# A Flamingo block on one core: statistics, scaling, transposes, routing and shared expert of each mixture put into one block, quad by quad

## What is computed

```python
x = x + tanh(g_xattn[0]) * L0_xattn(layernorm(x), ctx)
x = x + tanh(g_ffn[0])   * moe0(layernorm(x))      # stage b of the kernel
x = x + tanh(g_xattn[1]) * L1_xattn(layernorm(x), ctx)
x = x + tanh(g_ffn[1])   * block1(layernorm(x))    # stages d (attention) and e (mixture)

# moe0: 64 experts in 8 groups, 4 groups kept, 6 experts per token, and a shared expert
shared = silu(x @ sg_w.T) * (x @ su_w.T) @ sd_w.T
scores = sigmoid(x @ gate_w.T) + gate_bias
masked_scores = scores * mask_of_the_4_best_groups
topk_w, topk_i = top_k(masked_scores, 6); topk_w /= sum + 1e-8 ; comb = scatter(topk_w)
routed = einsum(silu(x eg) * (x eu), ed, comb)
# second half of block1: 8 experts, 2 per token, no shared expert
t = rmsnorm(x, g2); probs = softmax(t @ router_w); w = top2(probs) / sum
y = sum_e w_e * (silu(t w1_e) * (t w3_e)) w2_e ;  return res + y
```

## Time and profile before

| | us |
|---|---|
| median of 3 runs (2174.27 to 2177.08) | 2176.98 |
| the profiled execution | 2178.36 |
| its span (first to last instruction) | 2176.6 |
| PE busy | 1817.9 (84%) |
| DVE busy | 1544.9 (71%) |
| POOL busy | 1145.5 (53%) |
| ACT busy | 1067.9 (49%) |

### The profile page before, as it was taken

How to read it: one execution, slowest core, us unless ns; L and a number is a source line. 1 busy time by engine, 2 the same in 40 slices (tenths; PEclk the granted TensorE clock), 3 DMA queues, 4 the chain that set the end, 5 groups by cost and what they waited for, 6 DMA issues and landing times. The chain is left out here.

```text
span 2176.6 us, 40812 instructions
## 1 busy us (share of the span) xinstructions
PE 1817.9 (84%) x12306; PEld 1455.1 (67%) x12306; DVE 1544.9 (71%) x3089; ACT 1067.9 (49%) x2730; POOL 1145.5 (53%) x1146
## 2 busy tenths in 40 slices
PE   4677844699999999957999999994688884399998
PEld 3455533488888888846999999993444443388886
DVE  5698869477777777776666666665578785487776
ACT  2366632255555555534655665561256662255554
POOL 4666621476676677643333333334567762276664
PEclk9699965799999999977999999996889995599999
DMA  5111100355556555400000000000000000122222
GB/s 120 44 45 40 38 1 17 90 129 144 143 144 144 138 133 146 127 19 4 5 3 3 3 3 3 3 3 0 0 2 1 0 1 2 50 68 78 78 68 68
DMA packets 99989, 114.75 MB, mean 53 GB/s; under 512 B 18448, under 2 KB 55504, under 8 KB 99888
## 3 DMA queue, kind: packets, MB, share of 16 engines
q1 hardware_dynamic: 93888, 110.96, 19.8%
q10 hardware_dynamic: 6000, 2.57, 0.6%
HBM read 101.82 MB, written 3.28 MB: 48 GB/s over the span
## 5 line engine op out<-in xcount | busy, mean ns | idle before, releaser
L76 POOL TENSOR_TENSOR b_moe_hid_low<-b_moe_hid,b_moe_hid_high 128x512 fp32r<-128x512 f32 x256 | 331.4, 1295 | 168.1 <-ACT b_moe_hid_high L1007 166.4
L1013 ACT ACTIVATE bank<-bank 128x512 f32<-128x512 f32 x384 | 223.5, 582 | 368.4 <-PE bank L83 368.4
L1547 POOL TENSOR_TENSOR c_prob<-c_prob,c_recip 128x480 f32<-128x480 f32 x128 | 126.2, 986 | 308.0 <-DVE c_recip L1698 308.0
L1656 ACT ACTIVATE c_prob<-bank,c_shift 128x120 f32<-128x120 f32 x512 | 177.5, 358 | 183.2 <-DVE c_shift L1690 183.2
L1038 DVE TENSOR_TENSOR b_moe_gu<-bank,XC 128x512 f32<-128x512 f32 x256 | 176.7, 690 | 108.5 <-PE bank L83 107.4
L76 POOL TENSOR_TENSOR e_moe_hid_low<-e_moe_hid,e_moe_hid_high 128x512 fp32r<-128x512 f32 x128 | 165.7, 1295 | 84.4 <-ACT e_moe_hid_high L1007 83.6
L71 DVE CAST c_ts_high<-bank 128x480 fp32r<-128x480 f32 x128 | 84.9, 663 | 165.9 <-PE bank L1578 165.9
L1043 DVE TENSOR_TENSOR b_moe_hid<-bank,b_moe_gu 128x512 f32<-128x512 f32 x256 | 177.0, 691 | 8.8 <-POOL b_moe_hid_low L76 0.2
L1007 ACT ACTIVATE b_moe_hid_high<-b_moe_hid 128x512 fp32r<-128x512 f32 x256 | 159.9, 625 | 5.7 <-DVE b_moe_hid L1043 5.1
L1578 PE MATMUL bank<-c_cs,mT 96*128 96x120 f32 x1024 | 138.8, 280 | 6.2 <-POOL c_wvp_low L76 4.9
L1578 PEld LDWEIGHTS bank<-c_cs,mT 96*128 96x128 f32 x1024 | 133.1, 196 | 14.9 <-POOL c_wvp_low L76 5.3
(11 more groups left out here) (367 smaller groups left out, 5455.9 us busy)
## 6 DMA issues: line engine op xcount, KB each, us to landing
XC<-b_comb SPq DMA_DIRECT2D x256, 256.0 KB, 4.3
...
```

Source lines behind the costliest of these rows:

```text
L76: return eng.tensor_tensor(low.bitcast(F32R), x, high, ALU.subtract)
L1013: act.activation(gate_b[j % 4][:], gate_b[j % 4][:], ACT.Silu).then_inc(s_silu, 1)
L1547: pool.tensor_tensor(prob[k][:], prob[k][:], recip[:, k, :].unsqueeze(2).broadcast_to([P, HG, NKV]), ALU.mult).then_inc(s_norm, 1)
L1656: i = act.activation(prob[k][:, h, :], score_b[g % 2][:, h * NKV:(h + 1) * NKV], ACT.Exp, bias=shift[:, k, h:h + 1], accum_out=sums[:, k, ...
```

## The change

`stats`, `Norm` and `route` are replaced, for the two mixtures, by one function `settle` with one block. In it each quad goes through all its steps, and every loop is written out.

- DVE: `bn_stats` of quad t, `bn_aggr` of quad t-1, variance of quad t-2 (and mean square of quad t-3 in stage e), all eight quads; then the routing chain of the eight quads without anything between. The subtraction over 4096 columns and the scaling leave DVE. In stage b the addition of the bias and the last multiplication of the chain go to Pool, and "not equal" and "times" become one `scalar_tensor_tensor` (in stage e too).
- ACT: scales (in stage b with the shift as bias), four instructions a quad; then both copies of the quad before, and the sigmoid or exponential of the one before that. After all eight quads it turns to a second loop: `stage` copies and the shared expert's activations.
- Pool: per quad the power and (stage b) the shift, the low part, the bias addition, the last multiplication; then in the same list the shared expert's weights, its product and its low part. In stage e it adds Z (scaled by ACT) to X in eight pieces.
- PE: transposes and logits of all quads; then, quad by quad, the shared expert's first two products, the transposes of the routing weights, and the third product of the quad before. Gate and up have one PSUM bank each.
- SP: the four stores of routing weights of each quad, instead of ACT.

The diff, cut:

```diff
-        def route(tag, ctx, XT, combD, s_stored, norm, gateT, ne, logits_to_scores, comb):
...
+        def settle(tag, ctx, src, centred, gain, XT, combD, s_stored, gateT, ne, comb, scores, shared=None):
...
+                @block.sync
+                def _(sp):
+                    for q in range(NQ):
+                        sp.wait_ge(s_cc, q + 1)
                         for j in range(4):
                             per = P // width
                             rows = (j % per) * width
-                            act.dma_start(combD[:, bass.ds(q * 512 + j * P, P)],
-                                          stage[u][rows:rows + ne, (j // per) * P:(j // per + 1) * P]).then_inc(s_stored[u], 16)
-                    body(0, 0)
-                    body(1, 1)
-                    with stepped(act, 2, NQ, 2) as q:
-                        store_comb(q - 2, 0)
-                        body(q, 0)
-                        store_comb(q - 1, 1)
-                        body(q + 1, 1)
-                    store_comb(NQ - 2, 0)
-                    store_comb(NQ - 1, 1)
+                            sp.dma_start(combD[:, q * 512 + j * P:q * 512 + (j + 1) * P],
+                                         stage[q % 2][rows:rows + ne, (j // per) * P:(j // per + 1) * P])\
+                                .then_inc(s_stored[q % 2], 16)
                     for k in range(2):
-                        act.wait_ge(s_stored[k], 32 * NQ)
+                        sp.wait_ge(s_stored[k], 32 * NQ)
...
+                    for t in range(NQ + 3):
+                        if t < NQ:
+                            tile_stats(t)
+                        if 0 <= t - 1 < NQ:
+                            gather_stats(t - 1)
+                        if 0 <= t - 2 < NQ:
+                            variance(t - 2)
+                        if 0 <= t - 3 < NQ:
+                            mean_square(t - 3)
+                    dve_scores(dve)
...
+                    def roots(q):
+                        part = slice(4 * q, 4 * q + 4)
+                        pool.wait_ge(s_var, q + 1)
+                        pool.tensor_tensor(rstd[:, part], var[:, part], root[:], ALU.pow).then_inc(s_rs, 1)
+                        if centred:
+                            pool.wait_ge(s_rs, q + 1)
+                            pool.tensor_tensor(shift[:, part], negmean[:, part], rstd[:, part], ALU.mult).then_inc(s_shift, 1)
+                    def low_tokens(q):
+                        pool.wait_ge(s_xhigh, q + 1)
+                        pool.wait_ge(s_xs, q + 1)
+                        chunk = slice(q * 512, q * 512 + 512)
+                        keep_low(pool, XT[1][:, chunk], xs[q % 2][:], XT[0][:, chunk]).then_inc(s_xt, 1)
+                    roots(0)
+                    roots(1)
+                    for t in range(NQ + 7):
+                        if t + 2 < NQ:
+                            roots(t + 2)
+                        if t < NQ:
+                            low_tokens(t)
+                        pool_scores(pool, t - 1)
+                        if shared is not None:
+                            shared.gpsimd(pool, t - 6)
...
+                    def scale(q):
+                        u = q % 2
+                        act.wait_ge(s_rs, q + 1)
+                        if centred:
+                            act.wait_ge(s_shift, q + 1)
+                        wait(act, s_turned, q - 1)
+                        for j in range(4):
+                            b = 4 * q + j
+                            if centred:
+                                i = act.activation(xn[u][:, j, :], src[:, b, :], ACT.Identity, scale=rstd[:, b:b + 1],
+                                                   bias=shift[:, b:b + 1])
+                            else:
+                                i = act.activation(xn[u][:, j, :], src[:, b, :], ACT.Copy, scale=rstd[:, b:b + 1])
...
+                    def store_tokens(q):
+                        u = q % 2
+                        act.wait_ge(s_turned, q + 1)
+                        act.activation(XT[0][:, q * 512:q * 512 + 512].bitcast(F32R), turn_b[u][:], ACT.Copy,
+                                       **kw).then_inc(s_xhigh, 1)
+                        wait(act, s_xt, q - 1)
+                        wait(act, s_logit, q - 1)
+                        act.activation(xs[u][:], turn_b[u][:], ACT.Copy, **kw).then_inc(s_xs, 1)
+                    def stage_comb(q):
+                        u = q % 2
+                        act.wait_ge(s_ct, q + 1)
+                        wait(act, s_stored[u], (q - u) * 32)
+                        act.activation(stage[u][:], turned_comb[u], ACT.Copy).then_inc(s_cc, 1)
+                    for t in range(NQ + 2):
+                        if t < NQ:
+                            scale(t)
+                        if 0 <= t - 1 < NQ:
+                            store_tokens(t - 1)
+                        if 0 <= t - 2 < NQ:
+                            act_scores(act, t - 2)
+                    for q in range(NQ + 2):
+                        if q < NQ:
+                            stage_comb(q)
+                        if shared is not None:
+                            shared.scalar(act, q)
...
+                        pe.wait_ge(s_cb, q + 1)
+                        pe.wait_ge(s_xs, NQ)
+                        wait(pe, s_cc, q - 1)
...
+                    for t in range(NQ + 1):
+                        if t < NQ:
+                            turn(t)
+                        if 0 <= t - 1 < NQ:
+                            logits_of(t - 1)
+                    for q in range(NQ + 1):
+                        if shared is not None:
+                            shared.tensor_first(pe, q, s_xt)
+                        if q < NQ:
+                            turn_comb(q)
+                        if shared is not None:
+                            shared.tensor_second(pe, q - 1)
...
-        stats("b_stat")
...
+                    chain(dve.scalar_tensor_tensor(cw[q][:], mr[:, :, 0:E0], -BIG, ms[:, :, 0:E0], ALU.is_equal, ALU.mult))
+                    chain(dve.tensor_reduce(ssum[:, q, :], cw[q][:], AX.X, ALU.add))
+                    chain(dve.tensor_scalar(ssum[:, q, :], ssum[:, q, :], 1e-8, None, ALU.add))
+                    dve.reciprocal(ssum[:, q, :], ssum[:, q, :]).then_inc(s_rc, 1)
...
+            def pool_scores(pool, q):
+                if 0 <= q < NQ:
+                    pool.wait_ge(s_sig, q + 1)
+                    pool.tensor_tensor(sc[q][:], sc[q][:], gb0[:].unsqueeze(1).broadcast_to([P, 4, E0]), ALU.add).then_inc(s_sc, 1)
+                if 0 <= q - 2 < NQ:
+                    k = q - 2
+                    pool.wait_ge(s_rc, k + 1)
+                    pool.tensor_tensor(cw[k][:], cw[k][:], ssum[:, k, :].unsqueeze(2).broadcast_to([P, 4, E0]),
+                                       ALU.mult).then_inc(s_cb, 1)
...
+            gate_b, up_b, down_b = bank[4], bank[5], bank[6:8]
...
+            def gpsimd(cls, pool, t):
+                if t == -1:
+                    for k in range(3):
+                        keep_high(pool, sh_w[k][0][:], cls.weights[k][:]).then_inc(s_swh, 1)
+                        pool.wait_ge(s_swh, k + 1)
+                        keep_low(pool, sh_w[k][1][:], cls.weights[k][:], sh_w[k][0][:]).then_inc(s_swl, 1)
+                if 0 <= t < NQ:
+                    u = t % 2
+                    pool.wait_ge(s_sil, t + 1)
+                    pool.tensor_tensor(sh_up[u][:], sh_up[u][:], sh_gate[u][:], ALU.mult).then_inc(s_shp, 1)
+                if 0 <= t - 1 < NQ:
+                    u = (t - 1) % 2
+                    pool.wait_ge(s_shh, t)
+                    keep_low(pool, sh_low[u][:], sh_up[u][:], sh_high[u][:]).then_inc(s_shl, 1)
+            @classmethod
+            def tensor_first(cls, pe, q, s_xt):
+                if not 0 <= q < NQ:
+                    return
+                if q == 0:
+                    pe.wait_ge(s_swl, 3)
+                pe.wait_ge(s_xt, q + 1)
+                wait(pe, s_sil, q)
+                x_parts = [t[:, q * 512:q * 512 + 512] for t in XT]
+                split_product(pe, cls.gate_b[:], [t[:] for t in sh_w[0]], x_parts)
+                split_product(pe, cls.up_b[:], [t[:] for t in sh_w[1]], x_parts).then_inc(s_gu, 1)
+            @classmethod
+            def tensor_second(cls, pe, q):
+                if not 0 <= q < NQ:
+                    return
+                u = q % 2
+                pe.wait_ge(s_shl, q + 1)
+                wait(pe, s_sy, q - 1)
+                split_product(pe, cls.down_b[u][:], [t[:] for t in sh_w[2]], (sh_high[u][:], sh_low[u][:])).then_inc(s_sd, 1)
+            @classmethod
+            def scalar(cls, act, t):
+                if t < NQ:
+                    u = t % 2
+                    act.wait_ge(s_gu, t + 1)
+                    wait(act, s_sd, t - 1)
+                    act.activation(sh_gate[u][:], cls.gate_b[:], ACT.Silu)
```

(28 more changed lines are left out.)

394 lines of the change are left out of this document (166 added, 228 removed).

## The result

| | before | after |
|---|---|---|
| median, us | 2175.66 (2174.27 to 2177.08) | 2147.29 (2146.0 to 2148.76) |
| span of the profiled execution | 2176.6 | 2144.2 |
| ratio | | 0.987, 95% interval 0.9853 to 0.9887 |

The forecast was 2153 with 2138 to 2170. I cut the profiled executions at five marks: first statistic of stage b, first load of its experts, first statistic of stage e, first load of its experts, end.

A forecast was written before the change was run, and what follows sets the result against it. The prediction took stage b's routing to go at DVE's pace, and stage e's quads to go round DVE, PE and ACT. Savings of 8.7 us (b) and 15.4 us (e), together 24.1, gave 2153 us from 2176.98, range 2138 to 2170.

The forecast's parts named there:

- Stage b's head: Stage b, from the start of its statistics to the first routing chain step: 13.6 us.
- The chain: Stage b's routing on DVE: 5.1 us a quad plus 0.8 for collisions with Pool, so 5.9.
- Rivals 1 and 3: DVE's chain steps wait 0.6 or 1.1 us each for Pool: 2166 us (chance 0.20) or 2196 us (chance 0.08).
- The shared expert's start: Stage b: the shared expert begins 34.7 us in, after quad 2's multiplication and six weight steps on Pool.
- Its round: Stage b's shared expert: one quad at a time goes round PE, ACT and Pool, 8.5 us a quad.
- The clock: Stage b's shared loop: PE stays at 1.2 GHz throughout, working in bursts with idle time between.
- Rival 2: The clock rises in stage b's shared loop: 6.7 us a quad, 37.5 us saved in all, 2140 us; chance 0.15.
- Stage e: Stage e, from first statistic to first expert load: 58.5 us against 73.9, a gain of 15.4 us.
- To the first exponential: Stage e's head, by stage b's sum with DVE's last statistics ahead of the first reduction: 14.8 us.
- From there to the last exponential: Stage e's eight quads at the pace of DVE's chain, seven intervals of 3.74 us: 26.2 us.
- The tail: Stage e after the last exponential: weights copied and stored, 3.8 us for two quads; 17.5 us in all.
- The total: Stages b and e together save 24.1 us: span 2152.5 us, median 2153 us.

The follow-up runs named there:

- e3: The changed kernel with a second PSUM bank each for gate and up, and their products earlier in PE's list: 2146.49 us, stage b 102.5 us.
- e9: The changed kernel with ACT's and Pool's lists reordered in stage b's shared loop, finishing the previous quad's high and low parts first: 2125.62 us, stage b 82.5.
- e8: The changed kernel with eight idle matmuls per quad on PE, except the last, before the wait for the low part: 2132.76 us, stage b 92.5 us.
- e6: The changed kernel without Pool's addition of Z to X in stage e: 2144.62 us, stage e 45.9 us.

## Why the prediction was right, step by step

The walk through stage b's waits gave the right length, stage e's gain was forecast more than a third too small, and the total stayed in the range because the range was wide: by stage lengths the change is worth 33.3 us where the sum had 24.1.

- **Stage b's head**, 13.6 to the first chain step: 13.8 (312.54 less 298.7). The power of four columns was 1.01 us (forecast 1.0), the shift 0.20, a scaling pace 0.38 (0.35).
- **The chain**, 5.1 and 0.8 for meetings, 5.9: measured from 312.54 to the last quad's reduction at 352.2, 5.67 a quad, so 0.57 for meetings instead of 0.8, if the bare chain is the 5.1 of the sum. A single one, DVE and then Pool of after:

```profile
314.33 1.47 DVE L1377 TENSOR_TENSOR b_ms<-b_sc,b_gr 128x256 f32<-128x256 f32 x1
```

```profile
314.26 1.27 POOL L76 TENSOR_TENSOR b_XT_low<-b_route_xs,b_XT_high 128x512 fp32r<-128x512 f32 x1 [0.57 <-ACT b_route_xs L1259]
```

The step is 0.42 us long when alone (321.03). Here it began inside Pool's instruction and ended 0.27 us after it. Rivals 1 and 3 had the mechanism, and this is what their price would be on every step; but Pool was seldom in the way.
- **The shared expert's start**, 34.7: PE began at 333.21, which is 34.5.
- **Its round**, 8.5: 8.46, and this close an agreement is partly luck. The round shown is 8.65 us: Pool's product took 1.22 to the next start and not 1.0, and the other terms together 0.06 less than I had. In three of the six rounds the clock rose in the last matmuls, and they took 8.08 to 8.32. The cause that I named is wrong. I wrote that gate and up have one bank each and that PE does the third product of a quad before the first two of a later one. In e3 they have two banks and another place on PE, and the round stays; in e9 banks and PE's list stay, and the round opens when ACT's and Pool's lists are turned. The sum held because it added up the waits in the order in which the lists make them, with the low part behind Pool's product.
- **The clock**, 1.2 GHz: 0.61 in the mean of the loop and 0.50 elsewhere in the stage. It rose only at the end of some bursts, and was back at 1.2 GHz in the next. Rival 2's 6.7 us a round came out in e8, where PE was made busy.
- **Stage e** was underestimated by 9.2 us, in three terms. To the first exponential 11.6 us instead of 14.8: I had DVE's last statistics in front of the first reduction, but DVE was done with them and waited for PE's logits (after):

```profile
1817.55 0.19 DVE L1959 TENSOR_REDUCE e_max<-bank 128x4 f32<-128x32 f32 x1 [0.55 <-PE bank L1295]
```

The rest of these 3.2 us lies in what I carried over from stage b's sum without giving its terms, and can't be split. From there to the last exponential 24.5 instead of 26.2: DVE's chain was the right path, but I counted it seven times at 3.74. Two shifting steps stand ahead of the first chain, so the first interval was only 2.37 us (1817.78 to 1820.15), and that is 1.4 of the 1.7. The other six took 3.70 in the mean, 2.88 of the chain's own where I had 3.1 and 0.8 of meetings where I had 0.6: two errors that cancel. Pool I had at 3.6 and "just covered"; it is 3.45, without a gap in most quads. The tail 13.2 instead of 17.5: 4.3 us, of which 3 x (3.8 - 2.7) = 3.3 is the pace of the stores, since SP issues one in 0.295 us and lets ACT go on, where the earlier trace rows had ACT issuing.
- **The total.** The span is 2144.2 where the forecast had 2152.5: 9.2 of stage e, less 0.8 that the three untouched stretches added. The median is 2147.3 instead of 2153; the other 2.7 us are how a profiled execution stands to the medians of its runs.

Of the Trainium skill's two sentences, "SBUF — State Buffer", "Who interferes with whom", is borne out by the two lines above and by e6 (474 ns to 192 in the median, 3.46 us of the stage). "Perfetto Trace Analysis", "Optimizing Scalar/DVE Operations", warned that moving work from VectorE to GpSimd might not help. Here the whole change, of which this move is a part, took 8.7 and 24.6 us off; DVE had 84.8 us of work in stage b's 111.4, and Pool was idle for 79 of them. No run makes the move alone. Where it stops helping is seen in stage e, where Pool's addition costs 3.46 us by meetings and is still cheaper than the 4.49 us instruction at the end that it replaces.
